# W3's upper half loaded and used ahead of the fourth x tile, and VectorE's head chunks taken in another order, in a gated FFN kernel on one Trainium2 core

## The reference: what is computed

```
q_emb = relu(cond @ W3 + b3)                 # 64 x 512, W3 is 256 x 512
x1    = (n * x + sum_over_tokens(x)) * q_emb # n = 64
y     = relu(x1 @ W2 + b2)
base  = y @ W_base + b_base
h     = [router, A_s, A_r](y)                # 128 columns in all
gates = top2(softmax(router part + b_router))
out   = x + base + B_s part + gates * h @ B_r
```

## Time and profile before

| what | value |
| --- | --- |
| time, median of 3 runs | 236.16 us (236.14 to 236.66) |
| time of the profiled execution | 236.26 us |
| its span, first to last instruction | 234.1 us |
| granted TensorE clock, mean | 1.000 |
| PE busy | 229.5 us (98% of the span) |
| DVE busy | 165.8 us (71%) |
| ACT busy | 86.4 us (37%) |
| POOL busy | 48.9 us (21%) |
| DMA | 28.80 MB, mean 123 GB/s |

### The profile page before, as it was taken

The page is one execution under the profiler, slowest core; times in us unless marked ns, Lnnn a source line. Parts: engine busy times, 40 slices in busy tenths (PEclk is TensorE's granted clock), DMA queues, the critical chain, the costliest instruction groups (busy, mean ns, idle before and its releaser), DMA issues.

```text
span 234.1 us, 3090 instructions
## 1 busy us (share of the span) xinstructions
PE 229.5 (98%) x1007; PEld 188.3 (80%) x1007; DVE 165.8 (71%) x309; ACT 86.4 (37%) x171; POOL 48.9 (21%) x57
## 2 busy tenths in 40 slices
PE   7999999999999999999999999999999999999994
PEld 3977888888888888888888888888888888888883
DVE  0685979899889966596939969399656966064344
ACT  3178632646036330535116240263306351252430
POOL 6089334032212211013012211022111030000000
PEclk9999999999999999999999999999999999999999
DMA  6999903509270723626053641709020360104004
GB/s 207 313 229 229 276 5 79 137 3 315 67 187 4 250 111 69 144 107 255 10 134 69 194 167 26 185 4 345 12 34 0 141 218 14 21 0 179 3 0 179
DMA packets 32505, 28.80 MB, mean 123 GB/s; under 512 B 5817, under 2 KB 22909, under 8 KB 32494
## 3 DMA queue, kind: packets, MB, share of 16 engines
q1 hardware_dynamic: 30682, 28.50, 43.1%
q10 hardware_dynamic: 1812, 0.17, 0.6%
HBM read 18.89 MB, written 8.39 MB: 117 GB/s over the span
## 4 chain that ended last, share of the span: by engine, by line
PE 97%; DVE 1%; ACT 1%; issue 0%; DVEq 0%
PE m_ps L750 78%; PE hT L750 9%; PE m_ps L777 5%; PE m_ps L727 2%; DVE out_nat L628 1%; PE m_ps L740 1%; PE m_ps L769 1%; PE hT L740 0%; ACT qT L367 0%; ACT W_hi L373 0%; ACT x_hi L378 0%; PE m_ps L734 0%; DVE idle L468 0%; PE hT L877 0%; PE m_ps L733 0%
## 5 line engine op out<-in xcount | busy, mean ns | idle before, releaser
L308 POOL TENSOR_TENSOR x_full<-x_sum,qT 128x512 f32<-128x512 f32 x28 | 32.2, 1150 | 134.6 <-DVE x_sum L486 134.6
L353 ACT ACTIVATE y_hi<-m_ps,condT 128x512 fp32r<-128x512 f32 x32 | 22.0, 687 | 77.5 <-PE m_ps L750 77.2
L750 PE MATMUL m_ps<-Wb_lo,y_hi 128*128 128x512 f32 x128 | 49.8, 389 | 0.0
L750 PE MATMUL m_ps<-Wb_hi,y_lo 128*128 128x512 f32 x128 | 49.8, 389 | 0.0
L750 PE MATMUL m_ps<-Wb_hi,y_hi 128*128 128x512 f32 x128 | 49.8, 389 | 0.0
L750 PE MATMUL m_ps<-x_hi,W_hi 128*128 128x512 f32 x112 | 43.6, 389 | 0.0
L750 PE MATMUL m_ps<-x_hi,W_lo 128*128 128x512 f32 x112 | 43.6, 389 | 0.0
L500 DVE TENSOR_TENSOR y_lo<-m_ps,y_hi 128x512 fp32r<-128x512 f32 x32 | 21.6, 674 | 30.4 <-ACT m_ps L355 30.4
L750 PE MATMUL m_ps<-x_lo,W_hi 128*128 128x512 f32 x112 | 41.8, 389 | 0.0
L474 DVE STREAM_TRANSPOSE xT<-x_quart 128x512 f32<-128x512 f32 x28 | 30.3, 1083 | 0.0
L750 PEld LDWEIGHTS m_ps<-Wb_hi,y_hi 128*128 128x128 f32 x128 | 24.0, 188 | 5.0
(11 more groups left out here) (99 smaller groups left out, 256.5 us busy)
## 6 DMA issues: line engine op xcount, KB each, us to landing
out_dram<-out_nat SPq DMA_DIRECT2D x32, 256.0 KB, 2.2
x_quart<-in_x_dram SPq DMA_DIRECT2D x28, 256.0 KB, 4.5
x_nat<-in_x_dram SPq DMA_DIRECT2D x7, 1024.0 KB, 6.1
gatesT<-wT SPq DMA_DIRECT2D x28, 48.0 KB
x_nat<-in_x_dram SPq DMA_DIRECT2D x4, 256.0 KB, 3.7
W_f<-in_L_cond_W_dram SPq DMA_DIRECT2D x4, 256.0 KB, 6.7
Wb_f<-in_L_ffn_W_base_dram SPq DMA_DIRECT2D x1, 1024.0 KB, 9.2
W_sb<-in_L_cond_W_dram SPq DMA_DIRECT2D x2, 256.0 KB, 5.0
```

What stands on the lines that cost most here:

```text
L308: nc.gpsimd.tensor_tensor(per_batch(x1_full[:, c, :]), per_batch(x1_sum[:, c, :]), qT[:, c, bass.ds(BG * g, BG)].unsqueeze(2).to_broadcast ...
L353: nc.scalar.activation(y_hi[:, m, :], m1_ps[m][:, :], ACT.Relu, bias=b2_sb[:, m:m + 1]).then_inc(y_hi_ready, 1)
L750: mm = nc.tensor.matmul(psum, lhsT, rhs, start=start and i == 0, stop=stop and i == len(terms) - 1)
```

## The change: what it does

SyncE issues W3's first half (the code calls it load_W3(0)) ahead of the load of the fourth x tile, and the second half behind it. TensorE does q(0, c) for c = 0, 1, 2 ahead of the fourth tile's four transposes (turn_head(3)), and the constant WARM_HALF, the number of zero matmuls behind q(0, c), goes from 2 to 1. VectorE does scale_head(0) ahead of sum_head(1), and from there on each rest_head(c) stands ahead of scale_head(c + 1). ScalarE's and GpSimd's lists are as before.

```diff
-    WARM_LOAD, WARM_W3, WARM_HALF, WARM_Q = 8, 1, 2, 1
+    WARM_LOAD, WARM_W3, WARM_HALF, WARM_Q = 8, 1, 1, 1
...
+            def load_W3(k):
+
+                sp.dma_start(W3_sb[:, k, :], W3[k * P:(k + 1) * P, :]).then_inc(W3_loaded[k], 16)
+
             for t in range(TT):
+                if t == TT - 1:
+                    load_W3(0)
                 sp.dma_start(x_nat[0][:, t, :], x_groups[0][:, t, :]).then_inc(head_loaded[t], 16)
-            for k in range(QC):
-                sp.dma_start(W3_sb[:, k, :], W3[k * P:(k + 1) * P, :]).then_inc(W3_loaded[k], 16)
+            load_W3(1)
...
             sum_head(0)
+            scale_head(0)
             sum_head(1)
-            scale_head(0)
+            rest_head(0)
             scale_head(1)
-            rest_head(0)
             sum_head(2)
+            rest_head(1)
             scale_head(2)
-            rest_head(1)
             sum_head(3)
+            rest_head(2)
             scale_head(3)
-            rest_head(2)
             rest_head(3)
...
-            for t in range(TT):
+            def turn_head(t):
+
                 pe.wait_ge(head_loaded[t], 16)
                 for c in range(KC):
                     turn = nc.tensor.transpose(head_ps[c][:, t * P:(t + 1) * P],
...
+            for t in range(TT - 1):
+                turn_head(t)
             keep_warm(WARM_W3)
...
                 pe.wait_ge(W3_loaded[k], 16)
                 for c in range(KC - 1):
                     q(k, c)
+                if k == 0:
+                    turn_head(TT - 1)
                 keep_warm(WARM_HALF if k == 0 else WARM_Q)
```

## The result

The changed kernel takes 236.60 us (median of 20 runs, 236.03 to 237.23), the kernel before 236.06 (20 runs), 0.54 us less; the ratio is 1.0029, 95% interval 1.0021 to 1.0038, which is 0.68 us more (0.50 to 0.90). The profiled execution took 236.64 us with a span of 234.7, that of before 236.26 and 234.1.

The account below looks back on a forecast made before the run. TensorE, busy 229.5 of 234.1 us, was taken as the bound, so head delays reach the end. Lateness 0.64 at y_lo plus 0.12 for an uncovered weight load made 0.76: 236.16 + 0.76 = 236.9 us, range 236.0 to 237.4.

Parts of the forecast that it names:

- just at that bound: Whole kernel: the forecast loss lies at what a measurement can tell from no change, about 0.3%, 0.7 us.
- Its own signs of being wrong: Wrong if m1 ends less than 0.3 later, first relu isn't at 21.8, or a later wait swallows or adds.
- TensorE's list and the step sizes: Head: fourth tile at 9.01, m1 at about 12.26, 0.21 earlier; VectorE steps 0.72, 0.81, 0.61, 0.60.
- VectorE's chain: Head sums, rests and scalings: first scaling at 10.86, chunk 1 about 1.9 late, chunk 3 at 18.45, 1.15 late.
- Chunk 1 and chunk 3 as two paths to the same place: m1: waits for chunk 1's W2_lo (some 0.6) and chunk 3's x_lo each put TensorE about 0.5 behind.
- ScalarE's tail: After 18.04: first relu goes to 21.80, y_lo ready at 28.96, TensorE starts that matmul 0.64 behind.
- A later wait may absorb it, and the chain has none: After the head: the head's change comes out at the end one for one, no later TensorE wait absorbing it.
- VectorE's next-group work taken at nothing: Behind the head: VectorE's next-group work ends before the h_head it waits for, priced at nothing.
- The zero matmul's 0.21: TensorE's head: one zero matmul taken out; q(1, c) and qT start 0.22 earlier, m1 0.21 earlier.
- The loads at nothing: Head loads: W3's half lands about 7.0, fourth x tile about 7.5, both ahead of need; priced at nothing.
- the rival's own terms: Late-load rival: W3's half lands behind 7.77, each 0.1 us passed on; with 0.5 late 237.4; chance 0.10.
- The clock rival: TensorE's clock could fall from 2.4 to 1.2 GHz in m1, 10 matmuls costing 2 us: 239; chance 0.03.

Follow-up runs that it names:

- Experiment 8: Changed kernel with y_lo of chunk 3 ahead of the transpose of chunk 2 in group 1; 236.52 us, ratio 1.0026.
- experiment 2: Kernel before with VectorE's new order alone; loads, TensorE and zero matmuls as before; 236.70 us, ratio 1.0039.
- experiment 9: Changed kernel with W2's chunk 1 split early on ScalarE and chunk 3's reduce over 8 of 64 tokens; 236.22 us, ratio 1.0021.
- experiment 4: Changed kernel with ScalarE's split of W2's chunk 1 ahead of x_hi of chunk 1; 236.76 us, ratio 1.0046.
- experiment 11: Changed kernel again, unaltered, on the chip of the two short-reduce kernels, against the kernel before; 236.88 us, ratio 1.0054.
- experiment 1: Kernel before with one zero matmul instead of two behind the first half's q products; 235.89 us, ratio 1.0009.
- experiment 5: Kernel before with W3's first half loaded ahead of the fourth x tile, nothing else; 236.30 us, ratio 1.0012.
- experiment 10: Changed kernel with chunk 3's reduce over 8 of 64 tokens only, W2 not split early; 236.40 us, ratio 1.0027.
- experiment 6: Kernel before with ScalarE's W2_split(0) ahead of the first qT, VectorE's third sum before first rest, third rest before fourth scaling; 235.54 us, ratio 0.9985.
- experiment 7: Kernel before with those ScalarE and VectorE head moves, plus group 1's y_lo of chunk 3 ahead of chunk 2's transpose; 235.48 us, ratio 0.9996.
- experiment 3: Changed kernel with VectorE's old order; loads, TensorE's order and one zero matmul less stay; 237.83 us, ratio 1.0080.
- the third move: y_lo of chunk 3 ahead of chunk 2's transpose in group 1; added to two head moves 235.48 us, to the changed kernel 236.52 us.

## Why the prediction held, point by point

- **The outcome.** Forecast 236.9, measured 236.60 against 236.06; +0.76 forecast, +0.68 by the ratio (0.50 to 0.90; 0.54 by the medians) and on a second chip +1.3 (0.85 to 1.7) measured. The sign, the range and the size are right; "just at that bound" was too cautious, since with 20 runs of each kernel the loss is clear of no change. That the size fits so well is partly luck. With the rise of the clock made level, the two profiles' spans differ by 0.99 us (234.7 + 0.39 - 234.1): 0.71 of it was there at h's y_lo matmul, as forecast, and 0.28 came behind it, where nothing was forecast. Why the medians differ by less than that isn't shown; the moment of the rise, which moves single executions by as much, is known of the profiled ones only.
- **Its own signs of being wrong.** Two of them came true as they stand: TensorE ended m1 0.16 us later (less than 0.3), and the first relu was at 21.37 (not 21.8). Both are the early rise of the clock: with 0.39 added they are 0.55 and 21.76. The third, a later wait that adds, came true in earnest, at 55.27.
- **TensorE's list and the step sizes.** Right to 0.03 us once the clock's rise is taken out: fourth tile, m1's start, the four scalings, and VectorE's steps of 0.72, 0.81, 0.61 and 0.60. Experiment 8's profile, with its late rise, shows the first two without that correction, 0.07 and 0.05 early.
- **VectorE's chain.** Right, and shown: the order alone costs the whole (experiment 2), and work taken out of the chain brings time back (experiment 9, in which W2 is split early too, which alone did nothing in experiment 4). The forecast 1.15 us for the fourth scaling was 0.77 in the profile plus 0.39 of clock.
- **Chunk 1 and chunk 3 as two paths to the same place.** The loss at chunk 1 was 0.64 (forecast some 0.6) and the 0.12 of the uncovered weight load, so that TensorE came to chunk 2 0.57 late (forecast 0.5) with the clock made level, and taking the waits away moved them (experiment 4). Right, but for W2_hi's share, which I hadn't named.
- **ScalarE's tail.** First relu forecast at 21.80, found at 21.37, again 0.4 early with the clock; the wait for y_lo is there.
- **"A later wait may absorb it, and the chain has none", and VectorE's next-group work taken at nothing.** Wrong in part. I took VectorE and TensorE to be level again at h_head and put the rest at nothing. They aren't: TensorE met VectorE's lateness a second time at 55.27, for 0.15 us, and for 0.30 in experiment 11. How it got past h_head is below, under the hardware.
- **The zero matmul's 0.21.** The start of m1 in the changed kernel fits with it; by itself it gained nothing that could be measured (experiment 1), perhaps because W3's load then held the q products.
- **The loads at nothing.** Right for the changed kernel's first profile, too bold as a rule: the fourth tile had 5.3 us to landing, not 4.8, in experiment 5, and TensorE's weight load stood idle for W3's half, for 0.15 to 1.49 us, in the profiles of experiments 4, 9, 10 and 11, in all of which the clock had risen early. By the rival's own terms, landed behind 7.77, it came true in one of the eight profiles with that load (experiment 10, 7.9), so the chance of 0.10 was about fair for single executions.
- **The clock rival.** The changed kernel's 26 executions never had a mean granted clock under 0.999, and the forecast for it held. But it is nearer than its 0.03 says: a VectorE order with a gap of 1.40 us before m1 fell in 5 of 6, one zero matmul less without the fourth tile between the q products in 3 of 12, and kernels with both zero matmuls in 1 of 6 (experiment 2) and 2 of 24 (experiments 6 and 7).

## What to carry to other kernels

Moving a piece of work earlier on the waiting engine's behalf is priced at the end of the list it was moved past: here chunk 0's scaling was no earlier (10.89 with the clock made level, 10.84 before), and the fourth chunk's was 1.15 us later. When several waits hold an engine to the same place, find the chain that they share before removing one; the moves of experiment 6, which started m1 earlier and brought the fourth scaling 0.15 us nearer to the first sum (9.27 us instead of 9.42), gained, while the removal of the longest wait gained nothing. And read where TensorE's clock rises in each profile before comparing start times, since the difference can be that alone: 0.39 us in the changed kernel's first profile, 0.97 in its second (first q products at 6.80 instead of 7.77).

## What the runs showed of the hardware

- **The rise of the clock moves between executions.** In the profiles the x transposes came to the faster pace between about 5.0 and 7.0 us after the start, with the same instructions ahead of them. The Trainium skill, "TensorE: Matmul & The Clock Gate", section "What you observe", says that the transition varies from run to run; the traces agree. When it comes early, the next bound shows: the fourth tile was then 0.2 to 0.4 us late in kernels with the old order, experiments 2, 6 and 7, though not in experiment 1.
- **The fall hits single executions, and its price varies.** Against the median of the undisturbed ones it cost 0.5 to 1.3 us in experiment 1, nothing in experiment 2, 1.3 to 2.6 in experiment 3, 1.3 and 1.7 in experiment 7 and 0.5 in experiment 9. In the profiles the granted clock went from 1.00 to 0.50 between 10.7 and 13.8 us. Before it TensorE had run q products and zero matmuls, with its weight load idle for 0.21 us at most at the start of the q products in experiment 1 and 0.41 in experiment 2; in experiment 3 its weight load had stood idle for 1.40 us and in experiment 10, ahead of the q products, for 1.49. What brings it about stays open.
- **One VectorE operation lasts until GpSimd's ends.** The small subtraction for the logits (24 columns) took 0.66 us before and 1.04 in the changed kernel, and 0.18 in group 1 of both. Timelines of DVE and POOL, first of the kernel before:

```profile
30.84 0.66 DVE L551 TENSOR_TENSOR logit<-h_nat,lmax 128x24 f32<-128x24 f32 x1
...
30.16 1.29 POOL L314 TENSOR_TENSOR Wu_lo<-Wu_f,Wu_hi 128x512 fp32r<-128x512 f32 x1
```

and of the changed kernel:

```profile
31.16 1.04 DVE L556 TENSOR_TENSOR logit<-h_nat,lmax 128x24 f32<-128x24 f32 x1
...
30.87 1.30 POOL L319 TENSOR_TENSOR Wu_lo<-Wu_f,Wu_hi 128x512 fp32r<-128x512 f32 x1
```

Both end where GpSimd's operation ends (31.50 and 31.45; 32.20 and 32.17), and the other profiles show the same. Where the third move shifted the lists in group 1, the subtraction was caught there too; in experiment 8 it took 0.47 and ended at 58.57, GpSimd's operation at 58.54 (in experiment 7 0.36):

```profile
58.10 0.47 DVE L556 TENSOR_TENSOR logit<-h_nat,lmax 128x24 f32<-128x24 f32 x1
...
57.29 1.25 POOL L313 TENSOR_TENSOR x_full<-x_sum,qT 128x512 f32<-128x512 f32 x1 [4.38 <-DVE x_sum L491]
```

It isn't so for every operation: VectorE's in the head, which read a PSUM bank, keep their 0.68 to 0.70 us while GpSimd works. GpSimd's operation in the first group stands behind x_full, which VectorE's late sums release, so it moved by 0.71 us, and with it VectorE, though h_head itself came only 0.3 late. By the profile, this carried the lateness into group 1. The Trainium skill, "SBUF — State Buffer", section "Terms", says that VectorE and GpSimd share a port pair that one holds for its full instruction while the other blocks; for this subtraction the traces agree. No run moved GpSimd's operation of the first group away, so the link to the wait at 55.27 is read from the profile and not tested by itself.
